# The first layer's pipeline in four stages instead of five, and x loaded ahead of other inputs

## What is computed

```python
# layer 0
xn = layernorm(x)
a, b, c = sigmoid(xn @ Wa.T + ba), tanh(xn @ Wb.T + bb), sigmoid(xn @ Wc.T + bc)
state[t] = a[t] * state[t-1] + (1 - a[t]) * b[t];  s = c * state      # over the 512 positions
g = silu(gelu(xn @ binarize(w1).T + b1) @ binarize(w2).T + b2)
x = x + s * g
# layer 1
xn = layernorm(x)
ss = xn * rsqrt(mean(xn * xn) + 1e-6)                # RMS norm; its gains are folded into weights
k, v, q = projections of ss, 8 heads, chunks of 64 positions
s = memory attention: gradients of a two-layer memory, a momentum scan and a decay scan over the
    chunks, retrieval with q, RMS norm, gate = sigmoid(ss shifted by 63 positions @ w_gate)
e = argmax(xn @ centroids.T)                          # one of 8 experts for each position
g = silu(xn + sigmoid(best score) * expert_e(layernorm(xn)))
x = x + s * g
```

## Time and profile before

| | before |
|---|---|
| median of three runs | 1191.07 us |
| profiled execution | 1189.44 us |
| its span, first to last instruction | 1187.6 us |
| first layer's steps | 30.4 to 169.15 us |
| second layer | 169.15 us to the end |
| busy: PE, DVE, ACT, POOL | 93%, 61%, 57%, 47% of the span |
| mean granted TensorE clock | 0.965 of full speed |

### The profile page before, as it was taken

One profiled execution on the slowest core, in us unless ns is written; L12 is line 12 of the kernel. 1 busy time (PEld: TensorE's weight loads), 2 busy tenths in 40 slices (PEclk: granted clock), 3 DMA queues, 4 the chain that ended last, 5 costly groups with the idle time before them and its releaser, 6 DMA issues. The chain is left out here.

```text
span 1187.6 us, 20255 instructions
## 1 busy us (share of the span) xinstructions
PE 1100.7 (93%) x6649; PEld 917.9 (77%) x6650; DVE 720.1 (61%) x1892; ACT 679.8 (57%) x1369; POOL 561.9 (47%) x571
## 2 busy tenths in 40 slices
PE   4589869999999999999999899998999899999995
PEld 3356547788888888888888788887888788888884
DVE  4488856877655655655555455554555555556785
ACT  4666635566565565655555455554556455556663
POOL 3167753487764434444433343343434343344553
PEclk9888959999999999999999899999999999999998
DMA  9133330000300000000000000000000000002222
GB/s 209 38 89 90 89 115 1 1 21 21 98 24 1 2 16 10 10 10 18 9 10 7 20 8 10 8 9 19 8 8 9 19 8 10 3 5 77 88 88 72
DMA packets 57537, 40.32 MB, mean 34 GB/s; under 512 B 4595, under 2 KB 52061, under 8 KB 57310
## 3 DMA queue, kind: packets, MB, share of 16 engines
q1 hardware_dynamic: 53894, 32.10, 9.9%
q0 software_dynamic: 2304, 4.74, 1.2%
q10 hardware_dynamic: 1248, 2.23, 0.6%
HBM read 21.71 MB, written 15.50 MB: 31 GB/s over the span
## 5 line engine op out<-in xcount | busy, mean ns | idle before, releaser
L1105 DVE TENSOR_TENSOR p_sb<-bank,cf 128x512 f32<-128x512 f32 (+3 forms) x512 | 218.9, 483 | 1.1 <-PE bank L828 1.0
L1286 POOL TENSOR_TENSOR sq_rest<-sq,sq_high 128x450 f32<-128x450 f32 x64 | 67.2, 1050 | 247.1 <-ACT sq_high L995 247.1
L851 PE MATMUL bank<-p_sb,du_t 128*128 128x450 f32 (+3 forms) x512 | 131.1, 399 | 0.0
L851 PE MATMUL bank<-p_sb,err_t 128*128 128x450 f32 (+3 forms) x512 | 130.1, 397 | 0.0
L851 PEld LDWEIGHTS bank<-p_sb,err_t 128*128 128x128 f32 x512 | 85.0, 190 | 40.0 <-DVE p_sb L1105 16.9
L851 PEld LDWEIGHTS bank<-p_sb,du_t 128*128 128x128 f32 x512 | 82.0, 190 | 43.8 <-issue 29.8
L1138 DVE SCALAR_TENSOR_TENSOR acc<-bank,rg,acc 128x128 f32<-128x128 f32 x224 | 62.9, 344 | 84.6 <-POOL rg L1274 84.6
L1290 POOL TENSOR_TENSOR sq_low<-sq_rest,sq_mid 128x450 bf16<-128x450 f32 x64 | 66.6, 1041 | 100.1 <-ACT sq_mid L1012 99.9
L973 ACT ACTIVATE s_sb<-bank 128x512 f32<-128x512 f32 x64 | 38.3, 599 | 108.0 <-PE bank L828 108.0
L967 ACT ACTIVATE xs<-bank 128x450 f32<-128x450 f32 x64 | 35.1, 548 | 109.7 <-PE bank L851 108.5
L1174 DVE SCALAR_TENSOR_TENSOR du<-q_sb,bank 128x512 f32<-128x512 f32 x64 | 44.0, 688 | 87.5 <-PE bank L828 87.5
(11 more groups left out here) (304 smaller groups left out, 3193.0 us busy)
## 6 DMA issues: line engine op xcount, KB each, us to landing
x<-in_L_attn_inputs SPq DMA_DIRECT2D x16, 256.0 KB, 3.1
rows<-sorted_rows SPq DMA_DIRECT2D x40, 64.5 KB, 1.8
sorted_rows<-xl_all SPq DMA_DIRECT2D x1, 2064.0 KB, 14.7
x_rows<-x SPq DMA_DIRECT2D x8, 256.0 KB, 2.4
xn_rows<-xn SPq DMA_DIRECT2D x8, 256.0 KB, 2.4
xl_all<-xl SPq DMA_DIRECT2D x8, 256.0 KB, 3.4
ew<-in_L_ffn_w SPq DMA_DIRECT2D x8, 256.0 KB, 4.2
attn_out<-acc SPq DMA_DIRECT2D x7, 256.0 KB, 2.0
```

The lines of the kernel that those rows point to most:

```text
L851: last = pe.matmul(out[:, P * i:QW], rows[:, i, :], p_sb[:, P_COL[i]:P_COL[i] + QW - P * i], start=False, stop=True, skip_group_check=True)
L1105: last = nc.vector.tensor_tensor(dst, src, w, ALU.mult)
L1286: nc.gpsimd.tensor_tensor(sq_rest[:], sq[:], sq_3[0][:], ALU.subtract).then_inc(g_rest, 1)
```

## The change

**In prepare.** x of batches 0 and 1 is loaded ahead of `wcomb`. The fill counts on a semaphore that lives on (`m.s_filled`), its source lies in memory of the whole kernel, and SP no longer waits for it before the barrier: it waits as the first thing of layer0. ACT's chain for alpha (L216 to L221) stands right behind the two Signs instead of at the end.

**In layer0.** Stages b4 and b5 are one. y and xl are no longer made from xn1 but from x1 itself, by factors that follow from the variance of x1 alone: `ve1` has three rows of 4 columns, POOL takes one power of 12 columns, and the statistics of xn1, `ve2` and r2 are gone. `mv1` is double. nm now belongs to yt, whose four ACT instructions stand at the head of ACT's step, ahead of z and thg; xn of b1 is made by four POOL instructions (from x0 directly) and no longer by ACT, and the four gelus stand together. On POOL the order is r0, xn, xl, r1 (the 12 columns), high, low. The load of x1 on SP now waits also for yt and xl of two batches earlier, since they read x1. `w_sm` is 4 calls of 24 columns instead of 8, so the gate's columns come unshifted. There are 11 steps, steps 4 and 5 are the loop's body, and it is run twice, with one jump back.

**In attend.** The gate is shifted by 63 positions in head 0: two products with shift matrices (256 and 248 columns), PE waits for DVE's copy of the result. `count`, `blocks`, `places`, alpha's shift and the scatter come one head later each. `choose` has one multiplication more.

```diff
+                for b in range(2):
+                    sp.dma_start(m.x0[b][:], a["L0_attn_inputs"][b].rearrange("(k p) d -> p k d", p=P)).then_inc(m.s_x0[b], 16)
...
-                sp.dma_start(blocks[:, 0:NT, :], m.xl_all[:]).then_inc(filled, 16)
-                sp.dma_start(blocks[:, NT:, :], fill[:]).then_inc(filled, 16)
-                for b in range(2):
-                    sp.dma_start(m.x0[b][:], a["L0_attn_inputs"][b].rearrange("(k p) d -> p k d", p=P)).then_inc(m.s_x0[b], 16)
-                sp.wait_ge(filled, 32)
+                sp.dma_start(blocks[:, 0:NT, :], m.xl_all[:]).then_inc(m.s_filled, 16)
+                sp.dma_start(blocks[:, NT:, :], m.fill).then_inc(m.s_filled, 16)
...
-        ve0, ve1 = sb("ve0", [P, T]), sb("ve1", [P, T])
-        ve2 = sb("ve2", [P, 2, T])
-        r0, r1 = sb("r0", [P, T]), sb("r1", [P, T])
-        r2 = sb("r2", [P, 2, T])
+        ve0, ve1 = sb("ve0", [P, T]), sb("ve1", [P, 3, T])
+        r0, r1 = sb("r0", [P, T]), sb("r1", [P, 3, T])
...
+                        for taken in (v_xn1, c_yt, g_xl):
+                            sp.wait_ge(taken, less(b2.i, 1))
+                            sp.sem_inc(held_sp, 1)
+                        sp.dma_start(x1[q][:], x0_of(b2.i)).then_inc(s_x1[q], 16)
+                    if b4 is not None:
+                        q = b4.par
+                        sp.wait_ge(g_xl, b4.i + 1)
                         sp.sem_inc(held_sp, 1)
-                        sp.dma_start(x1[q][:], x0_of(b2.i)).then_inc(s_x1[q], 16)
-                    if b5 is not None:
-                        q = b5.par
-                        sp.wait_ge(g_xl, b5.i + 1)
-                        sp.sem_inc(held_sp, 1)
-                        sp.dma_start(m.xl_all[:, bass.ts(b5.i, T), 0:D], xl[q][:]).then_inc(s_xlo[q], 16)
+                        sp.dma_start(m.xl_all[:, bass.ts(b4.i, T), 0:D], xl[q][:]).then_inc(s_xlo[q], 16)
...
+                sp.wait_ge(m.s_filled, 32)
+                pipelined(sp, step, B, 4)
...
+                        pool.wait_ge(g_r0, b1.i + 1)
+                        pool.wait_ge(p_xn, b1.i)
+                        pool.sem_inc(held, 1)
+                        for k in range(T):
+                            last = nc.gpsimd.tensor_scalar(xn[:, k, :], x0[q][:, k, :], mv0[:, k, 0:1], r0[:, k:k + 1], ALU.subtract, ALU.mult)
+                        last.then_inc(g_xn, 1)
...
-                        pool.wait_ge(v_var2, b4.i + 1)
-                        pool.wait_ge(c_yt, b4.i)
-                        power(r2[:].rearrange("p a t -> p (a t)"), ve2[:].rearrange("p a t -> p (a t)"), 2 * T).then_inc(g_r2, 1)
-                        pool.wait_ge(g_r2, b4.i + 1)
+                        pool.wait_ge(g_r1, b4.i + 1)
...
-                            last = nc.gpsimd.tensor_scalar(xl[q][:, k, :], xn1[q][:, k, :], mv2[:, k, 0:1], r2[:, 1, k:k + 1], ALU.subtract, ALU.mult)
+                            last = nc.gpsimd.tensor_scalar(xl[q][:, k, :], x1[q][:, k, :], mv1[q][:, k, 0:1], r1[:, 2, k:k + 1], ALU.subtract, ALU.mult)
...
+                        pool.wait_ge(v_nm, b3.i)
+                        pool.wait_ge(c_yt, b3.i)
+                        pool.wait_ge(g_xl, b3.i)
+                        power(r1[:].rearrange("p a t -> p (a t)"), ve1[:].rearrange("p a t -> p (a t)"), 3 * T).then_inc(g_r1, 1)
...
+                        for k in range(T):
+                            pe.matmul(m.bank[7][:, 24 * k:24 * k + 24], y[:, k * P:k * P + P], m.w_sm[:], start=True, stop=True)
...
-                        for k in range(T):
-                            pe.matmul(m.bank[7][:, 24 * k:24 * k + 16], y[:, k * P:k * P + P], m.w_sm[:, 0:16], start=True, stop=True)
-                            pe.matmul(m.bank[7][:, 24 * k + 16:24 * k + 24], y[:, SHIFT + k * P:SHIFT + k * P + P],
-                                      m.w_sm[:, 16:24], start=True, stop=True)
...
+                        act.wait_ge(v_nm, b4.i + 1)
+                        act.wait_ge(p_y, b4.i)
+                        for k in range(T):
+                            nc.scalar.activation(yt[:, k, :], x1[q][:, k, :], ACT.Identity, bias=nm[:, k:k + 1], scale=r1[:, 1, k:k + 1])
+                        nc.scalar.copy(m.ry[:, :, bass.ts(b4.i, T)], r1[:, 0:2, :]).then_inc(c_yt, 1)
...
-                        for k in range(T):
-                            last = nc.scalar.activation(xn[:, k, :], x0[b1.par][:, k, :], ACT.Identity, bias=nm[:, k:k + 1], scale=r0[:, k:k + 1])
-                        last.then_inc(c_xn, 1)
...
+                        dve.wait_ge(g_r1, b4.i + 1)
+                        nc.vector.scalar_tensor_tensor(nm[:], mv1[q][:, :, 0], -1.0, r1[:, 1, :], ALU.mult, ALU.mult).then_inc(v_nm, 1)
...
-                        stats(link, xn1[q], mv2)
-
-                        link(nc.vector.tensor_tensor(ve2[:, 0, :], mv2[:, :, 0], mv2[:, :, 0], ALU.mult))
-                        nc.vector.scalar_tensor_tensor(ve2[:, 0, :], ve2[:, 0, :], RMS_EPS, mv2[:, :, 1], ALU.add, ALU.add)
-                        nc.vector.tensor_scalar(ve2[:, 1, :], mv2[:, :, 1], LN_EPS, None, ALU.add).then_inc(v_var2, 1)
...
+                        dve.wait_ge(g_r1, b3.i)
+                        stats(link, x1[q], mv1[q])
+                        var = mv1[q][:, :, 1]
+                        nc.vector.tensor_scalar(ve1[:, 0, :], var, LN_EPS, None, ALU.add)
+                        nc.vector.tensor_scalar(ve1[:, 1, :], var, 1.0 + RMS_EPS, LN_EPS * RMS_EPS, ALU.mult, ALU.add)
+                        nc.vector.tensor_scalar(ve1[:, 2, :], var, 1.0 + LN_EPS, LN_EPS * LN_EPS, ALU.mult, ALU.add).then_inc(v_var1, 1)
...
+                        pe.wait_ge(v_gate, 1)
+                        gate = m.gate_th[:].rearrange("p n e -> p (n e)")
+                        pe.matmul(QA[:, 0:NT * E], m.ahead, gate, start=True, stop=False)
+                        pe.matmul(QA[:, 0:(NT - 1) * E], m.behind, gate[:, E:], start=False, stop=True).then_inc(p_gate, 1)
+                        pe.wait_ge(v_moved, 1)
+                    if first_head(s) == 1:
...
+                    link(nc.vector.tensor_tensor(pos, pos, m.ry[:, 0, :], ALU.mult))
...
+                def moved():
+                    dve.wait_ge(p_gate, 1)
+                    nc.vector.tensor_copy(m.gate_th[:].rearrange("p n e -> p (n e)"), QA[:, 0:NT * E]).then_inc(v_moved, 1)
...
                         if c == 0:
-                            count()
+                            moved()
                         if c > 0:
                             coefs(c)
                         if c == 1:
+                            count()
...
+        m.s_filled = ctx.enter_context(nc.semaphore("s_filled"))
```

More of the change, by code:

```diff
@@ L130, in prepare @@
         got = {n: sem(f"got_{n}") for n in names}
-        filled = sem("filled")
         consts = sem("consts")
@@ L192, in _ @@
                 nc.scalar.activation(sg2[:], l0w2[:], ACT.Sign).then_inc(signs, 1)
+                act.wait_ge(signs, 2)
+                chain = Chain(act, act_c)
+                for k in range(FB):
+                    chain(nc.scalar.activation(l0w1[:, k, :], l0w1[:, k, :], ACT.Abs, accum_out=m.alpha1[:, k:k + 1]))
+                chain(nc.scalar.activation(l0w2[:], l0w2[:], ACT.Abs, accum_out=m.alpha2[:]))
+                chain(nc.scalar.mul(m.alpha1[:], m.alpha1[:], 1.0 / D))
+                chain(nc.scalar.mul(m.alpha2[:], m.alpha2[:], 1.0 / HF))
+                chain(nc.scalar.mul(m.alpha2h[:], m.alpha2[:], 0.5))
                 act.wait_ge(pe_group, 2)
@@ L250, in _ @@
                 chain(nc.gpsimd.iota(m.token_i[:], [[P, NT]], base=0, channel_multiplier=1))
-                for rows, n, first in ((m.xl_all, NT, 0), (fill, NB - NT, NT)):
+                for rows, n, first in ((m.xl_all, NT, 0), (m.fill, NB - NT, NT)):
                     chain(nc.gpsimd.memset(rows[:], 0.0))
@@ L427, in layer0 @@
         v_held, held, held_sp = sem("v_held"), sem("held"), sem("held_sp")
-        c1, c2, c3, c4, c5 = (sem(f"c{k}") for k in range(1, 6))
+        c1, c2, c3, c4 = (sem(f"c{k}") for k in range(1, 5))
         with nc.Block() as block:
@@ L669, in step @@
                         nc.vector.tensor_tensor(pr[:], st[:], z[:], ALU.mult).then_inc(v_pr, 1)
+                    if b4 is not None:
+                        y = m.y_f[b4.par]
+                        link = Chain(dve, c4, b4.i)
+                        dve.wait_ge(c_yf, b4.i + 1)
+                        link(nc.vector.tensor_reduce(cm[:], y[:, 0:S].rearrange("p (c n) -> p c n", n=C), AX.X, ALU.add))
+                        dve.wait_ge(c_sm, b4.i)
+                        nc.vector.scalar_tensor_tensor(cmw[:], cm[:].unsqueeze(2).broadcast_to([P, NC, 2 * H]), 1.0 / C,
+                                                       m.w_md[:].unsqueeze(1).broadcast_to([P, NC, 2 * H]), ALU.mult, ALU.mult).then_inc(v_cm, 1)
+                    if b3 is not None:
+                        q = b3.par
```

157 lines of the change are left out of this document (63 added, 94 removed).

## The result

The changed kernel is slower: 1197.61 us (median of seven runs, 1195.46 to 1201.34) against 1192.94 for the kernel before (seven runs in all, 1189.88 to 1194.64). The ratio is 1.0044, 95% interval 1.0026 to 1.0062. The forecast was 3.2 us faster; the change costs some 5 to 7.

The account below looks back on a forecast made before the run. PE was taken to bound the second layer and DVE to pace the first; -2.3 + 0 + 0.9 + 3.2 + 0.5 + 1.5 - 8.5 + 1.55 = -3.15 on the 1191.07 us median gave 1187.9, range 1183 to 1195.

Parts of the forecast that it names:

- the circle: First-layer loop: xl, three DMAs, x0's load, statistics, r0, xn, xl in series over SP and POOL; 14.1 us, 15.1 with slowdowns.
- Updates 3 to 6, the loop: Three steps between x1 updates in the first layer's loop, 42.1 us before; forecast +3.2 us at 15.1 a step.
- the break-even: Loop period at which the forecast gain of 3.15 us would be used up: 16.15 us.
- The circle becomes a wall: Rival: x0 lands 5 behind its issue or the jump costs POOL 4; 1191 to 1195 us, chance 0.17.
- Updates 6 to 8: Last two steps of the first layer, r1 standing behind xl on POOL; 25.5 us before, forecast 27.0, +1.5.
- First steps: First layer's steps with b1 and b2 alone, xn moved to POOL; forecast 0, with 0 to +1.4 us.
- Start: Prepare, up to the first statistics: without the wait for the fill they come at 28.1 for 30.37; -2.3 us.
- Tail: From the last x1 update to the second layer's first instruction: 12.2 us for 20.75, forecast -8.5.
- updates 1 to 3: Two early first-layer steps, 25.6 us before; DVE loses work but waits 2.0 a step for ACT; forecast +0.9 us.
- the shift: Head 0 of the second layer: PE stands still for the gate's new shift; forecast +1.55 us.
- The jump back: The first layer's loop now runs twice, with one jump; forecast +0.5 us, from 0 to 4.2.
- whole-instruction lock: Rival: DVE's two-input SBUF instructions each wait for a whole POOL instruction; step 18.8 us, time 1199 us, chance 0.05.

Follow-up runs that it names:

- e12: Changed kernel plus SP loading x0 a step ahead, POOL splitting y before the last update's power, DVE making nm before xn's low part: 1180.82 us.
- e13: Changed kernel with SP issuing x0's load behind x1's load but ahead of the stores of xl and x1: 1183.43 us.
- e2: Changed kernel with xn of the first stage back on ACT between its gelus, SP's order as changed: 1187.64 us.
- e3: Changed kernel with x0's load issued ahead of the previous step's three DMAs and xn back on ACT: 1187.04 us.
- e4: Kernel before the change, with only the change's part in prepare; the first layer keeps five stages: 1192.51 us.
- e5: Changed kernel with SP loading x0 a step ahead and POOL splitting y ahead of the 12-column power in every step: 1188.49 us.

## Why the prediction was wrong

- **The step that failed** is the price of the circle in *Updates 3 to 6, the loop*. The circle itself, its links in their order and the break-even were right: 15.1 + 3.15/3 = 16.15, and a turn came out at 17.0 for 15.1, inside the rival *The circle becomes a wall*, which had 0.17. Two terms were mis-sized. From the issue of x1's load to the statistics of the next x0 the sum has 1.6 of issue, 3.1 of landing and 0.35 for the fourth transfer, 5.05; it took 5.7 to 5.8 in the four turns of the first trace and up to 6.0 in the second. The fourth DMA was put 1.6 behind the first, from the spacing of 0.52 of a train that has only one store after two DMAs; it stood 2.2 to 2.7 behind, since 0.9 pass from the issue of the store of xl to the next, and 0.7 to 1.2 from that of x1. The landing with its wait took 3.1 to 3.6, the less the later x0 was issued, so only the sum of the two is a price. The landing of 5 that the wall named did not occur. And xl was priced at 3.14 + 0.3 wherever it may fall; behind xn it falls beside DVE's recurrence and takes 4.38. The two make 1.7 of the 1.9.
- **How far that goes.** With 17.0 in the loop and all else as forecast the sum would be -3.15 + 3 x 1.9 = +2.6, slower but within the range. In the second trace, 9.5 from the forecast, 5.4 lie in the loop with its jump, 1.5 in the first steps, 1.4 in the last updates, 1.0 in the tail and 0.5 in the start.
- **Updates 6 to 8.** I ended the circle with x0's last load. The step after it still starts from an r1 that stands behind xl on POOL: 17.1 and 15.8 in the two traces, where I had 15.7; the last one is 12.4 to 12.6, where I had 11.3. Missed 1.4 to 2.5. The 1.3 between the two traces go with the clock: in the step of 17.1 the products with `w_sm` and the transposes of pr took 1.90 and 1.09 at the lower level, in the other 1.07 and 0.63.
- **First steps.** Taken 0, measured +1.7 and +1.5. In step 0 xn on POOL is bare: PE's first transposes start 6.2 behind the first statistics instead of 4.7. But that is nearly all got back where the clock is as in the trace of before. e12 and e13, with POOL's xn too and a granted clock of 1.00 from 45 to 50 us, have 25.2 and 25.1 from there to the first update, for 24.8; after has 26.5 at 0.66. e2, e3 and e4, with xn on ACT and the clock at 0.51 to 0.66, have 26.5, 27.7 and 27.9. So the forecast of 0 to +1.4 was right in its mechanism, and some 1.3 of the +1.7 go with the clock in that execution.
- **Start.** -1.0 and -1.8 for -2.3: the mechanism was right, the first statistics stand 0.9 to 1.0 behind DVE's end, but that end moves by 2 us between executions.
- **Tail.** 13.25 for 12.2. The missing 1.1 is the split of the batch before, which stands between the power and xl in POOL's list (one of the rows printed ahead of the prediction) and which I left out of the sum; so the last xl lands behind ACT's end, what I had named as next in line (at 11.8, where 8.3 and 3.4 add to 11.7). e5 has 12.14 without it.
- **Right:** updates 1 to 3 (+0.9, measured +1.1), the twelve-column power (2.3, measured 2.29 to 2.67), the shift (1.55, measured 1.53), and the signs of the start, the loop, the last updates and the tail. That what makes updates 1 to 3 longer is DVE's wait for ACT, as I had it, no run tested alone.
- **The jump back** cost nothing that can be seen in the step over it: 16.9, its neighbours 16.9 to 17.2. This agrees with the rule of the Trainium skill (Runtime: NRT & Kernel Launch, Instruction fetch mechanics), and not with the 0.5 that I took. SP does show it: from the issue of x1's store to that of x0's load it has 1.18 in the turn over the jump (107.16 to 108.34) and 0.66 in the turns on either side, and x0 was taken up as soon behind the first issue as in those (5.8).
- **The port.** L491 took 4.38 beside DVE's recurrence and 3.12 away from it, so a contention of some 1.2 for four instructions exists (read from what runs beside it in each trace; no run changed DVE's work alone); it is less than the whole-instruction lock that I gave as a rival, and xn, beside z and pr, took 3.50.
- **The range** reached to 1195 and the time is 1197.6; 1.9 of that is the median of before, which was 1191.07 of three runs and is 1192.94 with four more. Against its own median the change, +4.7, lies 0.7 beyond the range's +3.9.

## What to carry to other kernels

When stages are merged and an engine is relieved, look for the circle that the new order closes across queues: write down, for each load, everything that stands ahead of it in its queue and what the last of these waits for. A load for the next step that stands behind a store of this step's last result puts the whole step in series; moving it ahead, or making that result first, cost nothing here and turned +0.5% into -1%. Price a queue by a row with the same sequence of DMAs, and an instruction at the place where it will run, beside what runs there then.
